# Decoder of twelve sublayers, regrouped self attention: sums over keys moved from VectorE's reductions to 16 accumulated unit-matrix products on TensorE

## The reference, cut to what matters

```python
def _L1_attn_ref(x, w_qkvw, w_out):
    H = 16
    G = 4
    DIM = 128
    HD = DIM // H // G
    B, S, dim = x.shape
    qkvw = x @ w_qkvw
    chunks = jnp.split(qkvw, G, axis=-1)
    subs = [jnp.split(t, G, axis=-1) for t in chunks]
    q = jnp.concatenate([subs[i][0] for i in range(4)], axis=0)
    ...
    def shp(t):
        return t.reshape(B * G, H, -1, HD).swapaxes(1, 2)
    q, k, v = (shp(q), shp(k), shp(v))
    w = w.reshape(B * G, H, -1, HD)
    scale = HD ** (-0.5)
    scores = q @ k.swapaxes(-2, -1) * scale
    attn = jax.nn.softmax(scores, axis=-1)
    o = (attn @ v).swapaxes(1, 2).reshape(B, S, dim)
    return o * w.reshape(B, S, dim) @ w_out
...
x = x + _L1_attn_ref(_layernorm(x, axis=-1), L1_attn_w_qkvw, L1_attn_w_out)
```

## Time and profile before

| | us |
|---|---|
| median of 3 runs | 1076.32 |
| lowest and highest | 1073.61 and 1080.63 |
| the profiled execution, its own time | 1071.34 |
| its span, from the first to the last instruction | 1069.5 |
| chunks of the regrouped attention, VectorE's first to last instruction | 355.28 to 425.22 |

### The profile page before, as it was taken

How to read it: one execution, slowest core, us unless ns; L and a number is a source line. 1 busy time by engine, 2 the same in 40 slices (tenths; PEclk the granted TensorE clock), 3 DMA queues, 4 the chain that set the end, 5 groups by cost and what they waited for, 6 DMA issues and landing times. The chain is left out here.

```text
span 1069.5 us, 18555 instructions
## 1 busy us (share of the span) xinstructions
PE 897.0 (84%) x6319; PEld 553.8 (52%) x6328; DVE 739.4 (69%) x2034; ACT 584.1 (55%) x1772; POOL 242.6 (23%) x357
## 2 busy tenths in 40 slices
PE   7998999999797272499679798986768999999997
PEld 4447999999465131345444486583752233333333
DVE  7658777777575698475778556515558888898953
ACT  5885777777333100243545344741443777777784
POOL 5013555555200122133030000351301111111110
PEclk8999999999999586699769999896885999999999
DMA  9600000000003600100001003550302101111000
GB/s 233 157 26 2 1 2 2 2 2 1 1 1 39 85 1 6 25 2 1 1 4 53 1 2 89 163 137 16 63 13 57 27 15 16 27 28 22 2 2 16
DMA packets 76186, 35.85 MB, mean 34 GB/s; under 512 B 35236, under 2 KB 74571, under 8 KB 76092
## 3 DMA queue, kind: packets, MB, share of 16 engines
q1 hardware_dynamic: 73724, 33.61, 14.1%
q0 software_dynamic: 896, 0.63, 0.2%
q10 hardware_dynamic: 1472, 0.41, 0.2%
HBM read 24.42 MB, written 11.05 MB: 33 GB/s over the span
## 5 line engine op out<-in xcount | busy, mean ns | idle before, releaser
L503 DVE TENSOR_REDUCE L3x_NMP<-L3x_pM 128x1 f32<-128x361 f32 x384 | 178.2, 524 | 19.9 <-PE L3x_pM L736 19.1
L657 ACT ACTIVATE L3x_E<-L3x_pS 128x400 f32<-128x400 f32 (+1 forms) x375 | 164.4, 509 | 47.4 <-PE L3x_pS L760 46.2
L736 PE MATMUL L3x_pM<-ctx_tm 64*128 64x361 bf16 x384 | 103.7, 340 | 13.9 <-DVE L3x_NMP L503 10.1
L760 PE MATMUL L3x_pS<-ctx_tm 64*128 64x400 bf16 (+1 forms) x375 | 105.4, 350 | 1.6 <-POOL ctx_tm L447 1.1
L1881 ACT ACTIVATE L0x_E<-L0x_E,ctx_r 128x100 f32<-128x100 f32 x288 | 105.0, 368 | 0.5 <-DVE L0x_E L1761 0.5
L736 PEld LDWEIGHTS L3x_pM<-ctx_tm 64*128 64x128 bf16 x384 | 30.2, 96 | 109.4 <-DVE L3x_NMP L503 90.3
L777 PE MATMUL L3x_pO<-L3x_E,CT 128*32 128x400 f32 (+1 forms) x768 | 85.1, 515 | 0.6 <-ACT L3x_E L657 0.4
L1690 POOL TENSOR_TENSOR L0x_E<-L0x_E,L0x_RZ 128x1200 f32<-128x1200 f32 x24 | 52.6, 2192 | 72.4 <-DVE L0x_RZ L1786 72.4
L2007 PE MATMUL L0x_pU<-ctx_tm,L0x_E 128*100 128x129 f32 x576 | 67.8, 273 | 1.1 <-POOL L0x_E L1690 1.1
L1995 PE MATMUL L0x_pS<-L0x_QS,CT 128*128 128x100 f32 x576 | 68.4, 275 | 0.0
L1995 PEld LDWEIGHTS L0x_pS<-L0x_QS,CT 128*128 128x128 f32 x576 | 66.2, 192 | 0.4 <-ACT L0x_QS L1873 0.4
(11 more groups left out here) (712 smaller groups left out, 2127.4 us busy)
## 6 DMA issues: line engine op xcount, KB each, us to landing
ctx_tm<-in_ctx SPq DMA_DIRECT2D x8, 704.0 KB
ctx_tm<-key_terms SPq DMA_DIRECT2D x16, 270.8 KB, 4.2
key_terms<-ctx_tm SPq DMA_DIRECT2D x42, 90.2 KB
ctx_tm<-in_L_ffn_wi SPq DMA_DIRECT2D x4, 512.0 KB, 7.8
ctx_tm<-in_L_ffn_wo SPq DMA_DIRECT2D x4, 512.0 KB
ctx_tm<-query_terms SPq DMA_DIRECT2D x16, 75.0 KB, 3.4
slots_in<-L2a_zeros SPq DMA_DIRECT2D x8, 129.0 KB
L2f_XS<-slots_in SPq DMA_DIRECT2D x4, 258.0 KB, 3.1
```

Source lines behind the costliest of these rows:

```text
L503: nc.vector.tensor_reduce(NMP[:, p, i // NC4, a, i % NC4:i % NC4 + 1], v, AX.X, ALU.max, negate=True).then_inc(s_mr, 1)
L657: nc.scalar.activation(E[0:r, n % EB, :], score_bank(n)[0:r, 0:NG * T], ACT.Exp, scale=SCALE8).then_inc(s_e, 1)
L736: nc.tensor.matmul(pM[:, n % 3, 0:CW], key_rows(QS, a)[:, b, p, 128 * x:128 * x + 128], key_rows(KS, a)[:, b % KB, c, p, :], start=True, s ...
L760: nc.tensor.matmul(score_bank(n)[0:NW[k], 0:NG * T], key_rows(KS, a)[:, b % KB, k % 4, p, 128 * (k // 4):128 * (k // 4) + NW[k]], key_rows ...
```

## The change

The three reductions on VectorE and the weighting on GpSimd go. E and the two weighted copies now lie side by side in one tile, `EW[128, 2, 3, STEP]` (two buffers, three parts, 1280 values with the keys innermost). VectorE makes both weighted copies. TensorE then sums over keys: 16 products with the f32 unit matrix, one for each key, all accumulated in one PSUM bank. The moving operand of each is the 3 x 80 = 240 values of one key, which lie 16 values (64 bytes) apart in EW. VectorE's closing part (`used`: a reciprocal, one product of 160 values that reads PSUM, and the two products with w) comes one chunk later in its order. TensorE does scores 2 before less_max 1, and gets 12 unread products ahead of scores 1. ScalarE's exponential of chunk n waits for the sums of chunk n-2 instead of for their use. OX moves into the free part of CT.

```diff
-        P0, P1, E = [buffers(B * 512 + 2 * i * STEP) for i in range(3)]
-        W0, W1 = s.sb("W0", [128, 2, STEP]), s.sb("W1", [128, 2, STEP])
+        P0, P1 = [buffers(B * 512 + 2 * i * STEP) for i in range(2)]
+        EW = s.sb("EW", [128, 2, 3, STEP])
+        E = EW[:, :, 0, :]
...
-            @block.gpsimd
-            def _(pool):
-                for n in range(N):
-                    pool.wait_ge(s_e, n + 1)
-                    pool.wait_ge(s_v, 1 if n == 0 else 2)
-                    if n >= 2:
-                        pool.wait_ge(s_o1, n - 1)
-                    nc.gpsimd.tensor_tensor(cube(W1[:, n % 2, :]), cube(E[:, n % 2, :]), kv(1, n, 1), ALU.mult)\
-                      .then_inc(s_w1, 1)
...
                 def weighted(n):
                     dve.wait_ge(s_e, n + 1)
                     dve.wait_ge(s_v, 1 if n == 0 else 2)
-                    nc.vector.tensor_tensor(cube(W0[:, n % 2, :]), cube(E[:, n % 2, :]), kv(1, n, 0), ALU.mult)\
-                      .then_inc(s_w0, 1)
-
-                def sums(n):
+                    if n >= 2:
+                        dve.wait_ge(s_sum, n - 1)
+                    for d in range(2):
+                        last = nc.vector.tensor_tensor(cube(EW[:, n % 2, 1 + d, :]), cube(E[:, n % 2, :]), kv(1, n, d),
+                                                       ALU.mult)
+                    last.then_inc(s_w, 1)
+
+                def used(n):
+                    dve.wait_ge(s_sum, n + 1)
                     if n >= 1:
                         dve.wait_ge(s_dn, n)
-                    chain.then(over_keys(den[:, :], E[:, n % 2, :], ALU.add))
-                    nc.vector.reciprocal(den[:, :], den[:, :])
-                    dve.wait_ge(s_w0, n + 1)
-                    chain.then(over_keys(OA[:, 0, :], W0[:, n % 2, :], ALU.add))
-                    dve.wait_ge(s_w1, n + 1)
-                    over_keys(OA[:, 1, :], W1[:, n % 2, :], ALU.add).then_inc(s_o1, 1)
-                    dve.wait_ge(s_o1, n + 1)
-                    for d in range(2):
-                        last = nc.vector.tensor_tensor(OA[:, d, :], OA[:, d, :], den[:, :], ALU.mult)
-                    chain.then(last)
+                    total = pT[:, n % 2, 0:3 * SUMS].rearrange("p (i x) -> p i x", i=3)
+                    chain.then(nc.vector.reciprocal(den[:, :], total[:, 0, :]))
+                    chain.then(nc.vector.tensor_tensor(OA[:, :, :], total[:, 1:3, :],
+                                                       den[:, :].unsqueeze(1).broadcast_to((128, 2, SUMS)), ALU.mult))
...
-                    sums(n)
+                    if n >= 1:
+                        used(n - 1)
+                used(N - 1)
...
-                        act.wait_ge(s_dn, n - 1)
+                        act.wait_ge(s_sum, n - 1)
...
+                def sums(n):
+                    pe.wait_ge(s_w, n + 1)
+                    if n >= 2:
+                        pe.wait_ge(s_dn, n - 1)
+                    by_key = EW[:, n % 2, :, :].rearrange("p i (x k) -> p k i x", k=NH)
+                    for key in range(NH):
+                        last = nc.tensor.matmul(pT[:, n % 2, 0:3 * SUMS], m.ident[:, :], by_key[:, key],
+                                                start=(key == 0), stop=(key == NH - 1))
+                    last.then_inc(s_sum, 1)
+
+                pe.wait_ge(s_k, 1)
+                unread_products(nc, m, pT[:, 1, :], 12)
                 scores(1)
+                scores(2)
                 less_max(1)
-                scores(2)
+                sums(0)
                 for n in range(2, N):
                     if n + 1 < N:
                         scores(n + 1)
                     less_max(n)
+                    sums(n - 1)
+                sums(N - 1)
```

More of the change, by code:

```diff
@@ L2305, in attention_regrouped @@
         mx = s.sb("mx", [128, 2, RC * NH])
-        den = s.sb("den", [128, RC * NH])
-        OA = s.sb("OA", [128, 2, RC * NH])
+        SUMS = RC * NH
+        den = s.sb("den", [128, SUMS])
+        OA = s.sb("OA", [128, 2, SUMS])
         O = s.sb("O", [128, NH, R, 2])
-        OX = s.sb("OX", [T, B, D])
+        at_free = B * 512 + 4 * STEP
+        OX = free[0:T, at_free:at_free + B * D].rearrange("t (b d) -> t b d", b=B)
         pA = s.ps("pA", [128, 8, 512])
@@ L2319, in attention_regrouped @@
         s_p, s_sc, s_mx, s_less = s.sem("products"), s.sem("scores"), s.sem("maxima"), s.sem("less_max")
-        s_e, s_w0, s_w1, s_o1, s_dn = [s.sem(x) for x in ("exps", "weighted_d0", "weighted_d1", "summed_d1", "used")]
+        s_e, s_w, s_sum, s_dn = [s.sem(x) for x in ("exps", "weighted", "summed_over_keys", "used")]
         s_o, s_od = s.sem("out_sbuf"), s.sem("out_in_dram")
```

## The result

The changed kernel takes 1107.45 us (median; 1105.73 to 1108.25), beside 1076.01 us for the kernel before: a ratio of 1.030, 95% interval 1.027 to 1.034. The profiled execution took 1107.69 us, 36.35 more than that of before; the medians are 31.4 apart, and their interval reaches from 29 to 36.

The account below looks back on a forecast made before the run. VectorE bound the chunks before, TensorE after; TensorE's dense list with S 14.4 shifts the end by +41.8 us, so 1076.3 becomes 1118 us. Forecast's own range 1108 to 1123; with (a) and (b), 1074 to 1124.

Parts of the forecast that it names:

- The bound moves to TensorE, and its list is dense: In the chunks TensorE replaces VectorE as the bound and works without a break from 365.7 to about 465.
- The step costs about twice the contiguous rate: In the sums, values 64 bytes apart cost TensorE 451 ns a pass instead of 0.20 us.
- S: TensorE's time for one chunk's sums, 32 passes: between 6.4 and 14.4 us, taken as 14.4.
- the prediction's formula: Shift of the end of VectorE's last product in the chunks: 5 S - 30.2 us, +41.8 with S 14.4.
- (a): Rival: TensorE reads stepped f32 values in the sums at full rate, S 6.4; 1078 to 1079 us; chance 0.32.
- (b): Rival: an in-between limit on the sums' stepped reads, S 8 to 12; 1086 to 1106 us; chance 0.08.
- Both rows give the same absolute figure: ScalarE's and VectorE's stepped reads both cost 1.88 ns a value, taken as a memory-side limit for TensorE's sums too.
- a surcharge of 0.85 ns on TensorE's own 0.83: Alternative for the stepped sums: only the extra time per value carries over to TensorE, giving S 12.9.
- VectorE's savings: In the chunks VectorE sheds 37.7 us and gains 16.5, so its busy time falls from 66.7 to about 45.5.
- I cost them at nothing: The 12 unread products ahead of scores 1 bring nothing; if the clock stays up, scores 1 saves 1.9 us.
- (c): Rival: stepped values fetched twice, S near 28.8, 1190 us; or sums lower the granted clock, 1139 us; chance 0.08.
- (d): Rival: VectorE remains the chunks' bound and the kernel wins up to 21 us; chance 0.02 with any other gain.

Follow-up runs that it names:

- experiments 3: Changed kernel with each sum product reading every fourth value (16-byte step), so it adds other values than the keys'; 1108.33 us, one run.
- experiment 4: Changed kernel with the sums made of bfloat16 upper halves at the same 64-byte step, 16 passes a chunk instead of 32; 1081.09 us, one run.
- experiment 1: Changed kernel with each sum product reading three contiguous pieces of 80 values, so it adds other values than the keys'; 1076.77 us, ratio 1.001 to before.
- experiment 5: Changed kernel with 12 unread f32 products at a 64-byte step ahead of scores 1, replacing the 12 unread bfloat16 ones; 1104.98 us, one run.
- experiment 6: Kernel before the change with GpSimd's weighting moved to VectorE, all else as before; 1081.15 us, ratio 1.003.
- Experiment 11: Changed kernel without its 12 unread bfloat16 products ahead of scores 1 and the wait ahead of them; 1108.96 us, ratio 1.029 to before.

## Why the prediction was right, and where its size was off

**The bound moves to TensorE, and its list is dense: right.** TensorE has no gap from 367.73 to the last sums. Scores 1 started at the lower clock and with `scores` 2 took 10.67 us, as worked out (6.40 + 4.27); experiments 3 and 4, 0.9 and 1.0 longer, show that this was not to be had to the tenth. The checks for waits held: `less_max` found each maximum ready.

**The step costs about twice the contiguous rate, and that decides: right, and shown** by experiment 1, in which only the addresses differ.

**The mis-sized term is S.** The prediction took 1.88 ns a value from ScalarE's and VectorE's stepped rows and so S = 14.4; TensorE needs 1.68 ns, and S is 12.93. With it the prediction's formula gives 5 x 12.93 - 30.2 = +34.5, and the stage grew by 34.6; 7.4 of the 41.8 us forecast were this term. The measured 1107.45 us is 10.5 under the 1118 of the sum and just under the forecast's own range of 1108 to 1123; it lies in the stated range because this reaches down for the rivals (a) and (b). (The 1123 should be 1121, by the sum's own terms: 1118 and 3 of spread.) The idea behind it, an absolute limit on the memory's side, held in kind: experiments 4 and 5 find the same 0.40 us a pass in both formats and at both clock levels. That it is the memory which sets this time is an inference; the runs show only that neither the format nor TensorE's clock does. "Both rows give the same absolute figure" was too strong, though. The two rows are of other engines and have another step, 200 bytes; no run tells which of the two makes them dearer. The prediction's other reading of the same rows, a surcharge of 0.85 ns on TensorE's own 0.83, gave S = 12.9. It was the right number by luck. A surcharge would make a bfloat16 pass 240 x (0.42 + 0.85) = 305 ns and an f32 pass at the lower clock 240 x (1.67 + 0.85) = 605 ns, and they take 403 and 405.

**VectorE's savings: right.** Its busy time in the chunks is 46.41 us (45.5 forecast), its weightings take 1.49 us each with no outlier, its product out of PSUM 0.32. That part of the old bound was contention with GpSimd is confirmed by experiment 6.

**"I cost them at nothing": not contradicted.** The 12 unread products end at 362.03 and TensorE waits 5.70 us. Experiment 11 is 0.6 us longer without them, less than the same two scores vary with them. Products that end 0.25 us before `scores` 1 bring 1.8 (experiment 5), the 1.9 that the prediction named.

**The rivals.** (a), full rate, is what experiment 1 makes of the kernel: 1076.77, 1.001; its price was right and its condition false. (b) gave S from 8 to 12 and 1086 to 1106 us, just under what came. Of (c), no pass took twice the limit (S is 12.93, not 28.8); but the granted clock did fall behind stepped passes in bfloat16 (experiment 4), though not in f32, where the window of the sums has 1.00. (d) is excluded: even with contiguous values TensorE stays the bound.

## What to carry to other kernels

Before moving a sum to TensorE, count the 16-byte lines that its moving operand touches: with one value a line, a pass took about 1.7 ns a column here, in both formats and at both clock levels, and the writer of the operand is the cheaper place for the step (1.1 us on the exponential against 6.45 on TensorE). When a stage's bound is traded for another engine's, compute that engine's dense list first, since 20 us saved on the old bound were worth nothing here. Then look at what follows TensorE's waits: products that nobody reads, ending just before the awaited work, gave 1.8 to 2.6 us in two places and nothing in a third, and products that ended 5.7 us early gave nothing that these runs can tell.

## What the hardware showed that I had not expected

- A fixed 1.68 ns for each value on a line of its own on TensorE's moving operand: 0.404 us for 240 f32 columns, 0.403 for 240 bfloat16 columns, 0.405 for f32 at the lower clock.
- A step of 8 bytes is nearly free (0.215 us a pass against 0.2025), and one of 16 bytes is dearer than one of 64 (0.424 against 0.404).
- In the bfloat16 run the granted clock fell to 0.76 behind the stepped passes, with TensorE busy throughout, and f32 `scores` took up to 5.76 us instead of 4.46. The runs don't show why bfloat16 passes do this and f32 ones of the same length don't.
